# New orders of three kinds of attention block on all engines, and a third place for split inputs, in an fp32 transformer kernel

## The reference

```
x = layernorm(x + attention(x))      # phase one: 16 heads, differential attention over all tokens
x = layernorm(x + transformer(x))    # phase two: 2 layers of local attention and gated feed-forward

layer(x):
    h = shift_token(x)                       # half of the channels from the token before
    q, k, v = split(h @ wqkv)                # 8 heads of 64
    q, k = rotary_xpos(l2norm(q) * qs, l2norm(k) * ks)
    o = local_attention(q, k, v)             # windows of 128 tokens, each sees itself and the one before
    x = x + o @ wo
    h = layernorm(shift_token(x)) * lg + lb
    a, g = split(h @ w1 + b1)                # 682 each
    x = x + (a * gelu(g)) @ w2 + b2
```

## Time and profile before

| | |
|---|---|
| median of 3 runs | 5556.42 us (5554.65 to 5564.04) |
| the profiled execution | 5557.89 us |
| its span, first to last instruction | 5555.8 us, mean granted TensorE clock 0.991 |
| PE busy | 5271.0 us, 95% |
| DVE busy | 4168.2 us, 75% |
| ACT busy | 3509.1 us, 63% |
| POOL busy | 1259.2 us, 23% |

### The profile page before, as it was taken

One profiled execution on the slowest core, in us unless ns is written; L12 is line 12 of the kernel. 1 busy time (PEld: TensorE's weight loads), 2 busy tenths in 40 slices (PEclk: granted clock), 3 DMA queues, 4 the chain that ended last, 5 costly groups with the idle time before them and its releaser, 6 DMA issues.

```text
span 5555.8 us, 150327 instructions
## 1 busy us (share of the span) xinstructions
PE 5271.0 (95%) x59592; PEld 2996.7 (54%) x59592; DVE 4168.2 (75%) x10819; ACT 3509.1 (63%) x7119; POOL 1259.2 (23%) x2489
## 2 busy tenths in 40 slices
PE   8999999999999999999789999999999999999997
PEld 3444444444444444544356666666666666666664
DVE  6888878888887888878567777777776777777774
ACT  4676667666666766767556566565565656656664
POOL 2222222222222222222212112111122121221211
PEclk9999999999999999999899999999999999999999
DMA  3333333233333333323110000000000000000000
GB/s 71 56 56 66 54 62 61 50 71 56 64 55 54 69 54 69 54 50 68 44 43 12 16 9 16 16 9 16 16 26 26 20 16 20 24 16 20 16 20 20
DMA packets 128829, 216.97 MB, mean 39 GB/s; under 512 B 40064, under 2 KB 40192, under 8 KB 127360
## 3 DMA queue, kind: packets, MB, share of 16 engines
q1 hardware_dynamic: 128128, 207.35, 18.4%
HBM read 46.78 MB, written 25.17 MB: 13 GB/s over the span
## 4 chain that ended last, share of the span: by engine, by line
PE 64%; ACT 15%; DVE 10%; issue 7%; POOL 4%; DMA 0%; POOLq 0%; ACTq 0%; SPq 0%; DVEq 0%
PE ps L617 23%; PE ps L746 14%; PE ps L1108 6%; PE ps L869 4%; ACT pt L1327 3%; PE ps L970 3%; PE ps L951 3%; PE ps L943 2%; ACT sm L1461 2%; DVE sm L1922 2%; ACT gates L1559 1%; PE ps L1049 1%; PE ps L1045 1%; PE ps L1046 1%; PE ps L927 1%
## 5 line engine op out<-in xcount | busy, mean ns | idle before, releaser
L1327 ACT ACTIVATE pt<-ps 128x1024 f32<-128x1024 f32 (+7 forms) x2048 | 1237.4, 654 | 620.1 <-PE ps L617 464.4
L746 PE MATMUL ps<-pt,va 128*32 128x512 f32 (+3 forms) x3072 | 1226.3, 487 | 22.3 <-POOL pt L2224 22.2
L746 PE MATMUL ps<-pt,ones 128*32 128x512 f32 (+3 forms) x6144 | 1236.3, 488 | 0.0
L746 PE MATMUL ps<-pt,vs 128*32 128x512 f32 (+3 forms) x3072 | 1230.0, 488 | 0.0
L1748 DVE CUSTOM_DVE_ANT_0 junk<-ps,causal 128x128 bf16<-128x128 f32 (+3 forms) x2048 | 978.1, 488 | 307.5 <-PE ps L617 291.7
L617 PE MATMUL ps<-kt,qt 96*32 96x512 bf16 (+3 forms) x12288 | 1017.4, 328 | 35.5 <-DVE mc L1748 16.3
L2224 POOL TENSOR_SCALAR_AFFINE_SELECT pt<-pt 128x256 f32<-128x256 f32 x1024 | 465.8, 455 | 1937.8 <-ACT pt L1327 1936.3
L617 PE MATMUL ps<-qt,kt 98*32 98x512 bf16 (+3 forms) x12288 | 836.6, 328 | 22.8 <-ACT pt L1327 22.0
L1752 DVE TENSOR_REDUCE mc<-ps 128x1 f32<-128x512 f32 x1024 | 706.4, 690 | 155.2 <-PE ps L617 124.5
L617 PEld LDWEIGHTS ps<-kt,qt 96*32 96x32 bf16 x12288 | 335.7, 94 | 578.4 <-DVE mc L1752 224.8
L1461 ACT ACTIVATE sm<-sm,mxw 128x256 f32<-128x256 f32 (+1 forms) x1024 | 494.0, 486 | 150.1 <-DVE mxw L1922 149.7
(11 more groups left out here) (170 smaller groups left out, 10221.6 us busy)
## 6 DMA issues: line engine op xcount, KB each, us to landing
qt<-part SPq DMA_DIRECT2D x768, 64.0 KB, 2.4
kt<-part SPq DMA_DIRECT2D x768, 64.0 KB, 2.5
ya<-wy SPq DMA_DIRECT2D x128, 128.0 KB, 2.3
yb<-wy SPq DMA_DIRECT2D x128, 128.0 KB, 2.3
xs<-between_phases SPq DMA_DIRECT2D x32, 512.0 KB, 3.8
xt<-in_x SPq DMA_DIRECT2D x16, 512.0 KB, 6.2
between_phases<-z SPq DMA_DIRECT2D x16, 512.0 KB, 2.8
between_phases<-xo SPq DMA_DIRECT2D x16, 512.0 KB, 2.7
```

Of the source, the lines that this page charges most:

```text
L746: mmi = pe.matmul(ps[32 * q:32 * q + 32, 4 + half, lo - half * 512:hi - half * 512], w, probs(kb)[:, i, lo - first(kb):hi - first(kb)], st ...
L1327: act.activation(probs(kb)[:, i, kb * P - first(kb):1024 - first(kb)], ps[:, 2 * i:2 * i + 2, :].rearrange("p a q -> p (a q)")[:, kb * P:1 ...
```

## The change

It gives xh and xl three places in place of two. It writes new orders of blocks 0, 2 and 3 on PE, ACT and DVE; block 1 keeps its order on these three. POOL splits the inputs at the start of each turn of its loop, before the low parts of the normalised inputs and before its own combine, and the two sums of the last layer norm's mean change places with the sum for the layer norm within the layer. In blocks 0 and 3 the transposes of head pair 0 go behind the keys' product and those of the others move by a product or so; ACT takes the squares ahead of the first copy. In block 0 DVE does the final addition behind the residual. In block 2 the scores of head pairs 2 and 3 go ahead of the values product, ACT does exponentials 2 and 3 ahead of the Gelu, and PE does all transposes of probabilities between whole hidden tiles. The arithmetic is the same. The diff, cut to its core:

```diff
-        xh = sb("xh", [P, 2, 2, P], F32R)
-        xl = sb("xl", [P, 2, 2, P], F32R)
+        xh = sb("xh", [P, 3, 2, P], F32R)
+        xl = sb("xl", [P, 3, 2, P], F32R)
...
@@ PE, block 0 @@
                     scores(W, 2)
                     scores(W, 3)
-                    transpose_p(W, 0)
                     keys(W + 1, 0)
                     keys(W + 1, 1)
+                    transpose_p(W, 0)
                     values(W, 0)
                     values(W, 1)
                     if W % (nb * WIN) == 4:
                         weigh_bias(W // (nb * WIN))
+                    transpose_p(W, 1)
                     attention_out(m, 0, (0,), True)
-                    transpose_p(W, 1)
                     attention_out(m, 0, (1,), True)
                     attention_out(m, 0, (2,), True)
+                    attention_out(m, 0, (3,), True)
                     transpose_p(W, 2)
-                    attention_out(m, 0, (3,), True)
...
@@ PE, block 2 @@
                     keys(W + 1, 1)
+                    scores(W, 2)
+                    scores(W, 3)
                     final_variance(m - 1, W)
                     transpose_p(W, 0)
                     values(W, 0)
                     values(W, 1)
                     transpose_p(W, 1)
-                    scores(W, 2)
-                    scores(W, 3)
-                    hidden(m, 0, True, (0,))
-                    hidden(m, 0, True, (1,))
-                    hidden(m, 1, True, (0,))
-                    hidden(m, 1, True, (1,))
-                    hidden(m, 2, True, (0,))
-                    hidden(m, 2, True, (1,))
-                    hidden(m, 3, True, (0,))
-                    hidden(m, 3, True, (1,))
-                    hidden(m, 4, True, (0,))
+                    hidden(m, 0, True)
+                    hidden(m, 1, True)
+                    hidden(m, 2, True)
                     transpose_p(W, 2)
+                    hidden(m, 3, True)
+                    transpose_p(W, 3)
+                    hidden(m, 4, True)
+                    transpose_q(W + 1)
                     weigh(W, 0)
-                    transpose_p(W, 3)
                     weigh(W, 1)
+                    transpose_k(W + 1)
                     weigh(W, 2)
-                    transpose_q(W + 1)
-                    hidden(m, 4, True, (1,))
-                    transpose_k(W + 1)
                     weigh(W, 3)
...
@@ PE, block 3 @@
-                    transpose_p(W, 0)
                     keys(W + 1, 0)
                     keys(W + 1, 1)
+                    transpose_p(W, 0)
                     values(W, 0)
                     values(W, 1)
+                    transpose_p(W, 1)
                     ffn_out(m, 0, (0,), True)
                     ffn_out(m, 0, (1,), True)
                     ffn_out(m, 0, (2,), True)
-                    transpose_p(W, 1)
+                    transpose_p(W, 2)
                     ffn_out(m, 0, (3,), True)
                     ffn_out(m, 0, (4,), True)
                     ffn_out(m, 0, (5,), True)
-                    transpose_p(W, 2)
                     ffn_out(m, 1, (0,), True)
+                    transpose_p(W, 3)
                     ffn_out(m, 1, (1,), True)
-                    transpose_p(W, 3)
...
@@ ACT, block 0 @@
                     exps(W, 1)
+                    squares(W + 1)
                     place_p(W, 0)
                     exps(W, 2)
-                    exps(W, 3)
-                    squares(W + 1)
+                    inverse_norms(W + 1)
                     values(W)
                     place_p(W, 1)
-                    inverse_norms(W + 1)
+                    exps(W, 3)
...
@@ ACT, block 2 @@
                     place_p(W, 0)
                     values(W)
+                    exps(W, 2)
+                    exps(W, 3)
+                    place_p(W, 1)
                     inverse_norms(W + 1)
                     gelu_table(m)
                     gelu(m, 0)
...
                     gelu(m, 5)
-                    exp_table(m)
-                    exps(W, 2)
-                    exps(W, 3)
-                    place_p(W, 1)
                     place_p(W, 2)
                     place_p(W, 3)
+                    exp_table(m)
...
@@ ACT, block 3 @@
                     exps(W, 1)
+                    squares(W + 1)
+                    place_p(W, 0)
                     exps(W, 2)
-                    place_p(W, 0)
-                    squares(W + 1)
                     inverse_norms(W + 1)
...
@@ DVE, block 0 @@
                     largest(W, 3)
-                    final_add(m - 1)
                     normalise(W, 1)
+                    norms(W + 1)
+                    rotate_own(W + 1)
                     normalise(W, 2)
+                    rotate_other(W + 1)
                     normalise(W, 3)
                     if W % (nb * WIN) == 4:
                         add_bias(W // (nb * WIN))
-                    norms(W + 1)
-                    rotate_own(W + 1)
-                    rotate_other(W + 1)
                     combine(W + 1)
                     residual(m, 0)
                     residual(m, 1)
+                    final_add(m - 1)
                     centre(m)
...
@@ DVE, block 2 @@
                     normalise(W, 1)
+                    largest(W, 2)
+                    largest(W, 3)
                     norms(W + 1)
                     rotate_own(W + 1)
                     rotate_other(W + 1)
-                    largest(W, 2)
-                    largest(W, 3)
                     gated(m, 0)
-                    final_normalise(m - 1)
+                    normalise(W, 2)
                     gated(m, 1)
+                    normalise(W, 3)
                     gated(m, 2)
-                    normalise(W, 2)
-                    normalise(W, 3)
                     combine(W + 1)
                     gated(m, 3)
                     gated(m, 4)
                     gated(m, 5)
+                    final_normalise(m - 1)
...
@@ POOL @@
-                if W >= 2:
-                    pool.wait_ge(v_full, done(W - 1))
+                if W >= 3:
+                    pool.wait_ge(v_full, done(W - 2))
...
             for W in range(LAST):
                 m = half_of(W)
+                split_x(W + 2)
                 if m >= 0 and W % 4 == 1:
                     inputs_low(m)
                 if W + 1 < LAST:
                     combine(W + 1)
-                split_x(W + 2)
...
                 if m >= 0 and W % 4 == 0:
+                    sum_channels(m)
                     final_channels(m - 1)
-                    sum_channels(m)
                     sum_squares(m)
```

More of the change, by code:

```diff
@@ L868, in project @@
                 for i, (v, w) in enumerate(((xh, wqh), (xl, wqh), (xh, wql))):
-                    mmi = pe.matmul(ps[:, bank, :], v[:, W % 2, kc, :], w[:, kc, cols],
+                    mmi = pe.matmul(ps[:, bank, :], v[:, W % 3, kc, :], w[:, kc, cols],
                                     start=kc == 0 and i == 0, stop=kc == 1 and i == 2)
@@ L2288, in split_x @@
                     pool.wait_ge(xs_ready[w // 4], sent(lb + 1))
-                if W >= 2:
-                    pool.wait_ge(v_full, done(W - 1))
+                if W >= 3:
+                    pool.wait_ge(v_full, done(W - 2))
                 for kc in range(2):
                     at = w * P + 1 - kc
-                    i = pool.tensor_copy(xh[:, W % 2, kc, :], xs[:, kc, at:at + P])
+                    i = pool.tensor_copy(xh[:, W % 3, kc, :], xs[:, kc, at:at + P])
                 i.then_inc(xh_done, 1)
@@ L2297, in split_x @@
                     at = w * P + 1 - kc
-                    i = pool.tensor_tensor(xl[:, W % 2, kc, :], xs[:, kc, at:at + P], xh[:, W % 2, kc, :], ALU.subtract)
+                    i = pool.tensor_tensor(xl[:, W % 3, kc, :], xs[:, kc, at:at + P], xh[:, W % 3, kc, :], ALU.subtract)
                 i.then_inc(xl_done, 1)
@@ L2329, in _ @@
                     final_sum_squares(m - 1)
+                if W == nb * WIN - 2:
+                    split_wqkv(1, 0)
+                    split_wqkv(1, 1)
+                if W == nb * WIN - 1:
+                    split_wqkv(1, 2)
             m = half_of(LAST)
+            sum_channels(m)
             final_channels(m - 1)
-            sum_channels(m)
             final_sum_squares(m - 1)
```

5 lines of the change are left out of this document (removed).

## The result

The changed kernel takes **5604.79 us**, median of 4 executions (5603.86 to 5605.74), against 5555.53 for the kernel before (5553.0 to 5564.04, 4 executions): a ratio of **1.0086 [1.0068, 1.0103]**, slower by 48 to 49 us. The forecast was 5579 with a range of 5545 to 5606. The direction was right and the range holds the time, at its upper edge; the size is more than twice the +22 forecast.

The account below looks back on a forecast made before the run. PE, busy for 95% of the span, was taken to bound the kernel. Block 2 +18, clock +28, block 3 -9, block 0 -14, once only -1 sum to +22 us: 5579 us, range 5545 to 5606.

Parts of the forecast that it names:

- Block 2's order: In block 2, hidden tile 2 starts later behind Gelu; +0.5 us a block (layer 0), +0.65 (layer 1), +18 us.
- The clock term: PE's new idle before hidden tile 2 halves the granted clock 23 times in 31 blocks, 1.2 us each: +28 us.
- The rule of the Trainium skill: By its abstract idle length no gap of the rounds lowers the clock; clock term 0, time 5551 us.
- Block 0: Block 0 (attention output product): DVE's chain ends earlier; whole windows -0.52 and -1.1 us, first +0.14 and -0.2; -14 us.
- The end: Behind the last window, final sum behind the residual and PE's final mean ahead of the next mean: +2.2 us.
- Block 3: Block 3 (second product): transpose of head 0 behind the keys' product hides waiting for sm; -0.28 us a block, -9 us.
- Windows 0 to 3: Window 2 carries no feed-forward work; its 2.76 us wait goes with no Gelu to pay: -2.5 us.
- That the clock holds: Rival: idles before hidden tile 2 are seldom followed by a fall; sum -6 us, 5551 us; chance 0.18.
- the faster one: Rival: idle ahead of hidden tile 2 is 2.4 us, the clock holds; -19 on top of -6, 5532 us; chance 0.14.
- The heavier rival: Rival: nearly every block 2 idle brings a fall (+12) and block 0's gains don't come (+14); 5605 us; chance 0.16.
- The signs named: Second phase: hh wait over 35 us, ptw nearly gone, sm halved, clock about 0.97, block 2 +1.5 us, block 3 -0.3.

Follow-up runs that it names:

- The filled idle: The changed kernel with ten added matmuls of 512 columns, result unread, between hidden tiles 1 and 2 in block 2: 5573.25 us, ratio 1.0036.
- the run with block 2 undone: The changed kernel with block 2 on PE, ACT and DVE in the order of the kernel before: 5553.17 us, ratio 0.9983.
- the one with the late steps mended: The changed kernel with block 2 as before, DVE's final addition behind centring, POOL's final sum later, old order after the last window: 5542.14 us, ratio 0.9968.
- block 2 alone: The kernel before with only block 2's new order on PE, ACT and DVE: 5612.35 us, ratio 1.0094.
- the final addition later: The changed kernel with DVE's final addition behind the centring and POOL's final sum behind the sum of squares: 5601.37 us, ratio 1.0074.

## Why the prediction was right in direction and short in size

**Block 2's order: right.** The step of the prediction put hidden tile 2 at 12.42 us behind the block's start (3461.83 to 3474.25); it came at 12.36 (3388.12 to 3400.48). The idle is 3.10 us in layer 0 and mostly 2.7 in layer 1, where I said 2.8 to 3.0. The block without a fall is 0.41 us longer in layer 0 and 0.54 in layer 1, against +0.5 and +0.65: +15 us against +18. The filled idle measured the same +15.4 by itself.

**The clock term: the right mechanism, mis-sized, and the largest miss.** I put down "23 x 1.2 = +28 us". There were 26 falls for 39 us. The number of falls was nearly met, in part by luck: it differs between kernels with the same idle (26, 21 and 21), and my three in four came from six idles. The price was not: one fall costs 23.31 - 21.95 = 1.36 us in layer 0, which is close to the raw 1.45 us read behind the fall at 4078. I had taken 0.2 us off because the wait for rr would swallow part, but block 2 of the new order has no wait for rr left to swallow it. And 4 of the 26 falls (windows 14, 38, 62 and 106) last longer, 6.8 us at half clock, and cost some 2.5 us each. I gave such a one no price: 22 x 1.36 + 4 x 2.5 = 40, close to the 39 measured. The trace before could have warned me, since two of its falls behind long idles last longer still, 10.2 us behind the idle of 3.31 us at 2808.38 and 15.2 us behind the 3.44 us of the earlier trace rows, though with further waits inside.

The rule of the Trainium skill (TensorE: Matmul & The Clock Gate, the section on how HAM oscillation bites in real kernels), by its abstract length of idle, left the clock up and gave 5551. The trace disagrees: idles of 2.7 to 3.1 us brought falls in 21 to 26 of 31 places, and idles of 2.0 to 2.4 us in 18. The mechanism that the same section describes, a stall that comes back in every round and pays for the fall again each time, is what happened, in 26 of 31 rounds.

**Block 0: right in layer 0, wrong in layer 1.** Layer 0 gave -3.9 us against -3.2. In layer 1 I had -1.1 us for whole and -0.2 for first windows, -10.4 in all. In the 14 windows behind window 68 it was -0.63 and +0.54, together about -0.6 where I had -9.1. The other 3.7 of the -4.3 us come in windows 64 (1.2) and 68 (2.5), and 1.6 of these are luck, the shorter fall in window 68. The step that failed reads: the final addition "goes behind the residual, where DVE waits for PE's mean anyway". DVE does wait there. But POOL doesn't: that is the moment of its sum, for which PE's mean waits, and the addition slows it from 1.27 to 2.17 us. I had looked for work queued behind the moved instruction on its own engine, and not for what another engine does at the same time. With the addition later, the same windows are at -1.21 and -0.36, which is what I had forecast and a little more, and layer 1 is at -13.0 in all.

**The end.** The same kind of step: final sum behind the residual, priced at +2.2, measured +4.7; with the old order there, 84.2 us from window 127 against 88.7. The mechanism was right and the wait behind POOL's final sum, 4.25 us, was sized too small.

**Block 3: right in kind, 0.2 us in place of 0.28 a block.** Of the -9 us, -5 came. I did not follow where the remaining 0.1 us a block stays.

**Windows 0 to 3.** I had -2.5 for the wait in window 2. That wait for ptw did go, but another took its place. The kernel after:

```profile
2789.07 0.66 PE L951 MATMUL ps<-identf,sm 128*128 128x128 f32 x4 [1.92 <-DVE sm L1927]
```

and the granted clock behind it, before and after:

```profile
2790.00:2798.00 8.00, 6.99 (x60) 4.68 (x58) 3.17 (x3) 4.20 (x7) 0.00 (x0) 1.00 0.00 0
```

```profile
2790.00:2798.00 8.00, 5.91 (x50) 4.65 (x52) 2.20 (x2) 2.69 (x6) 3.60 (x6) 0.79 0.00 0
```

The wait is shorter (1.92 us for 2.76), but two more follow it closely, 0.78 us at 2790.50 and this one, in which the clock fell (at 2792.4):

```profile
2792.72 1.12 PE L918 MATMUL ps<-identf,rr 128*128 128x128 f32 x4 [1.59 <-DVE rr L1909]
```

The three sum to 4.3 us; before, where the clock held, the waits in that stretch were 2.76, 0.19 and 0.69. I had followed the one wait and not what stood behind it. Window 2 takes 19.50 us for 18.04. In the run with block 2 undone windows 0 to 3 took 84.4 us, and 87.5 in the one with the late steps mended, though both have the same orders there; so these few windows also differ by execution.

**The rivals.** That the clock holds, and the faster one, are out. The heavier rival's time, 5605, is what was measured, but that is luck in half of its reasons: falls behind nearly every idle, yes; block 0 without its gain, no, since 8 of 15 us came. All misses but block 2's order lie on the same side, some 30 us, and less the 3 us of that order they make the 26 us between forecast and result. **The signs named** came out: hh over 35 us in each layer, ptw nearly gone, sm down from 12.4 to 7.9 us in layer 0; the clock from 2712 us to the end at 0.97 as forecast, 0.99 before; block 2 longer by 53.9 / 31 = 1.7 us on average, where I said 1.5; block 3 shorter by 0.2, not 0.3.

## What to carry to other kernels

When an order is rewritten so that many small waits go, follow the longest chain of the new order to the bottleneck engine and ask what that engine has left to do meanwhile: here the waits of 0.4, 1.12 and 0.19 us of a block had cost less than the one of 3.1 us that took their place, and only the long one was followed by a lower clock. Such an idle could be made harmless for the clock here with work that was ready anyway, and it needed only to be shortened (to 1.5 us, or to 1.7 with added matmuls), not closed. And when an operation is moved to where its own engine is idle, look at what the other engines run in that stretch: here DVE's addition lengthened POOL's sum from 1.27 to 2.17 us, and PE waited for that sum.

## What the runs showed of the hardware that I had not expected

- The step between the idles is narrow and not strict. In the same place, idles of 3.1 us brought a fall in 11 to 14 of 18 blocks, of 2.7 us in 7 to 12 of 13, of 2.4 us in 15 of 18, of 2.0 us in 3 of 13, and of 1.7 us and less in none. Yet at the start of phase two the clock held behind 2.76 us in one trace, and fell during a wait of 1.59 us in the other, behind waits of 1.92 and 0.78 us. The length of one idle alone doesn't decide; what else does is open.
- Some falls last 6.8 us and not 3.4. Over the kernel after, block 2 alone and the final addition later, these are 4, 3 and 7 falls at hidden tile 2, and all 14 began 0.61 to 0.91 us ahead of the tile's first matmul, still in the idle. The 54 short ones in the same traces began at 0.54 us ahead of it or later. Why stays open.
- DVE and POOL. DVE's addition began at 4492.81 and kept its 1.22 us, POOL's sum began 0.16 us later and took 2.17 us for 1.27. In the other case POOL's sum began first, at 4383.08, and kept 1.28 us, and DVE's addition 0.70 us later took 1.66 for 1.22. So it is the later of the two that pays, either way. The Trainium skill says this of the port that the two share (SBUF — State Buffer, the section on the two separate sides): whichever starts first has it for the whole instruction. The trace agrees on who pays. It falls a little short of full blocking: counted from the end of the first, the second needed 1.11 and 1.08 us more, less than the 1.27 and 1.22 it takes alone.
- 310 matmuls whose result nobody reads made this kernel 28 to 41 us faster: TensorE stayed at 2.4 GHz at hidden tile 2 in all 31 blocks, where it had fallen to 1.2 GHz in 26.
